# Graph network with LSTM windows: unit 0's gate products ahead of stream 1's last graph product, and two gates ahead of two tanh

## The chip, the cores and the metric

One core of one Trainium2 chip runs the kernel. The metric is the device time in microseconds (us) of one execution; lower is better.

## The reference, cut to what matters

`x` is [64 batches, 128 nodes, 128 features]. Two layers follow one another, each on a layer norm with relu of its input and each added to its input.

```python
h = relu(adj @ (h @ Wg0 + bg0))            # two graph layers, per batch
h = relu(adj @ (h @ Wg1 + bg1))
for p in range(1, 5):                      # windows of p nodes
    wins = h[:, :nw * p, :].reshape(Bv * nw, p, Hd)
    last = lstm_last(Wih[p-1], Whh[p-1], bih[p-1], bhh[p-1], wins)
    h = h.at[:, arange(nw) * p + (p - 1), :].set(last)
# one step of the LSTM:
g = x_t @ Wih.T + h @ Whh.T + bias         # i, f, g, o
c = sigmoid(f) * c + sigmoid(i) * tanh(gg)
h = sigmoid(o) * tanh(c)
# second layer, J = 128 nodes: diagonal, upper and lower part of adj,
# each with weights of its own, summed, plus a bias
```

The windows of one p are independent of one another; those of the next p read what this p wrote.

## The kernel before, in words

The 64 batches run as four groups of 16, and a group as two streams (s = 0, 1) of 8 batches. Every engine has its program written out by hand and waits for semaphores; no planner orders it. The instructions of an engine run in the order of its program.

The graph layers are four products per stream, named after their functions on TensorE: `graph_u` (L418), `graph_z` (L431), `graph_y` (L446) and `graph_v` (L456). Between them other engines take the product out of PSUM: VectorE adds a bias after z (`bias_z`, L910) and after y (`bias_y`, L918). After v, the last product, ScalarE writes the relu rounded to fp32r into HH (`high_h`, L732), and VectorE writes the rest, relu minus HH, into HL (`low_h`, L926). HH and HL together are the LSTM's input. Each of these works on a stream's two banks one after the other.

The LSTM is a list of 22 units, `UNITS` (L32). A unit is one step j of the windows of one p in one stream. For p = 1 each stream has two units of 64 windows (512 columns): units 0 and 2 are stream 0, units 1 and 3 stream 1. Units 4 and 5 are the first step of p = 2, units 6 and 7 the second, and so on. Unit 1 (as unit 0) is the first of its stream: on TensorE (`unit`, L464) it waits for both banks of HH before its first product and for both banks of HL before its third (L470 to L473, L504 to L506).

A unit of p = 1 has three gates (I, C, O; for the first step F is not needed), each of three products of 512 columns: HH by the weights' high part (L500), HH by their low part (L501), HL by the high part (L509). Each gate has its PSUM bank. ScalarE takes gate after gate (L829: sigmoid, or tanh for C, with a bias) into GT and then the tanh of the cell, CS into TC (L835). VectorE computes the cell between them (`unit_cell`, L936; I times C for a first step, L944), then out of the tanh the new hidden value: HH (L977) and HF (L978) for the last step of a window, and HL as HF minus HH (`unit_low`, L992). In group 0, the first, a gate of a new p or chunk waits on ScalarE until the HF of its stream's unit before is written (L812 to L815).

The order on VectorE for the units k (L1106 to L1131): the cell of k unless it was taken early, the hidden value of k, the cell of k + 1 if k + 1 is in `CELL_EARLY` (units 1, 2 and 15), then HL of k. So the cells of units 1 and 2 stand ahead of the HL of units 0 and 1, and the cell of unit 3 behind the HL of unit 2.

TensorE in group 0 starts unit 4 once the HH of unit 2 is written and unit 5 once that of unit 3 is (L491 to L493). Ahead of unit 4 it runs six filling products of ones (L484, 12 records in the profile), which nobody reads.

The stretch around the change, at the start of group 0, before:

- TensorE: y(0), v(0), y(1), v(1) (L621 to L624), then units 0, 1, 2, ...
- ScalarE: HH of stream 0, HH of stream 1 (L803, L804), then the gates and the tanh of unit 0, of unit 1, ...
- VectorE: Y(0), the first bank of HL(0), the first of Y(1), the second of HL(0), the second of Y(1), HL(1) (L1081 to L1086), a wait for the other groups' x (L1087), then the units.

In groups 1 to 3 the units of ScalarE and TensorE run with a plan, an argument that is None in group 0 alone; pieces of the second layer stand between their gates.

Of the kernel before, what the change touches and what calls it, by code (L numbers as in the profile page):

```python
# [9 lines left out]
ACT = mybir.ActivationFunctionType  # L10
# [3 lines left out]
GROUPS = B // G  # L14
HB = G // 2
# [3 lines left out]
HBANKS = HB // PACK  # L19
# [12 lines left out]
def lstm_units():  # L32


    units = []
    for p in SKIPS:
        chunks = max(1, (T // p) * HB // 512)
        nw = (T // p) // chunks
        for c in range(chunks):
            for j in range(p):  # L40
                for s in range(STREAMS):
                    units.append((p, s, j, c * nw, nw, FIRST_STEP if j == 0 else LATER_STEP))
    return units


UNITS = lstm_units()
# [83 lines left out]
LATE_ORDER = ("wi", "wh", "wl", "bias")  # L130

CELL_EARLY = (1, 2, 15)


LN_STATS_AT = {3: range(0, 3), 5: range(3, 5), 6: range(5, 9), 10: range(9, 12), 11: range(12, G)}
# [3 lines left out]
FIRST_STATS_AT = {4 + k: range(3 * k, min(3 * k + 3, G)) for k in range(6)}  # L139
# [5 lines left out]
def program(nc, x_tbd, adj_t, adj_diag, wg0, bg0_col, wg1, bg1, wih_t, whh_t, bih_t, bhh_t, w_l1, bias, out_tbd):  # L145
    with ExitStack() as ctx:
        def sb(name, shape, dt=F32):
            return ctx.enter_context(nc.sbuf_tensor(name, shape, dt))
# [20 lines left out]
        CS = sb("CS", [128, STREAMS, 512])  # L169
        IC = sb("IC", [128, STREAMS, 512])  # L170
        TC = sb("TC", [128, STREAMS, 512])
# [42 lines left out]
        x_rest = sem("x_rest")  # L214
# [34 lines left out]
        cell_ready = sem("cell_ready")  # L249
        tanh_ready = sem("tanh_ready")  # L250
# [20 lines left out]
        def bank(s, n):  # L271
            return PS[:, 4 * s + n, :]
# [144 lines left out]
        def _(pe):  # L417
# [26 lines left out]
            def graph_y(s, g):  # L444

                for n in range(HB):  # L446
                    if n % PACK == 0:
                        pe.wait_ge(h1_ready, 2 * HBANKS * g + s * HBANKS + n // PACK + 1)
                    mm = pe.matmul(as_batches(bank(s, 2 + n // PACK))[:, n % PACK, :],  # L449
                                   Z[:, s, T * n:T * n + T], WG1[:, :], start=True, stop=True)  # L450
                    if n % PACK == PACK - 1:
                        mm.then_inc(y_mm, 1)

            def graph_v(s, g):

                for n in range(HB):  # L456
                    if n % PACK == 0:
                        pe.wait_ge(y_sb, 2 * HBANKS * g + s * HBANKS + n // PACK + 1)
                    mm = pe.matmul(as_batches(bank(s, n // PACK))[:, n % PACK, :],  # L459
                                   Y[:, s, D * n:D * n + D], ADJ[:, :], start=True, stop=True)  # L460
                    if n % PACK == PACK - 1:
                        mm.then_inc(v_mm, 1)
# [158 lines left out]
            graph_y(0, 0)  # L621
            graph_v(0, 0)
            graph_y(1, 0)
            graph_v(1, 0)  # L624

            def units(i, plan):
                for k in range(len(UNITS)):
                    unit(k, i, plan)

            def next_graph(i):  # L630
# [26 lines left out]
            i = GROUPS - 1  # L657
# [54 lines left out]
        def _(act):  # L712
# [19 lines left out]
            def high_h(s, g):  # L732

                for n in range(HBANKS):
                    act.wait_ge(v_mm, 2 * HBANKS * g + s * HBANKS + n + 1)
                    act.activation(HH[:, s, :, n * PACK:(n + 1) * PACK],
                                   as_batches(bank(s, n)).rearrange("p b t -> p t b"),
                                   ACT.Relu).then_inc(h_high, 1)
# [45 lines left out]
            def last_copy(piece, g):  # L784

                if piece.what == TURN:
                    turn_up(g, piece.n, bank(piece.s, F))
                elif piece.what == VALUE:
                    copy_value(g, piece.n, bank(piece.s, F))
# [11 lines left out]
            relu_z(0, 0)  # L801
            relu_z(1, 0)
            high_h(0, 0)  # L803
            high_h(1, 0)  # L804
            act.wait_ge(bias_ready, 1)

            def unit(k, i, plan):

                p, s, j, w0, nw, gates = UNITS[k]
                prev = last_unit(k, s)  # L810
                n = nw * HB
                if plan is None and j == 0 and prev is not None:  # L812


                    act.wait_ge(lstm_step, STEPS * i + STEPS_BEFORE[prev] + STEPS_OF[prev])  # L815
                elif p == 1 and prev is not None:


                    act.wait_ge(lstm_step, STEPS * i + STEPS_BEFORE[prev] + STEPS_OF[prev] - 1)
                if plan and j > 0:  # L820

                    for m in range(len(gates)):
                        for piece in plan.at.get((k, m), ()):
                            last_copy(piece, i - 1)
                for m, q in enumerate(gates):
                    for piece in plan.at.get((k, m), ()) if plan and j == 0 else ():
                        last_copy(piece, i - 1)
                    act.wait_ge(gate_mm, GATES * i + GATES_BEFORE[k] + m + 1)
                    act.activation(GT[:, s, q, 0:n], bank(s, q)[:, 0:n],  # L829
                                   ACT.Tanh if q == C else ACT.Sigmoid,  # L830
                                   bias=BG[:, 4 * (p - 1) + q:4 * (p - 1) + q + 1]).then_inc(gate_act, 1)
                for piece in plan.at.get((k, len(gates)), ()) if plan else ():
                    last_copy(piece, i - 1)
                act.wait_ge(cell_ready, len(UNITS) * i + k + 1)
                act.activation(TC[:, s, 0:n], CS[:, s, 0:n], ACT.Tanh).then_inc(tanh_ready, 1)  # L835

            def units(i, more, plan):
                for k in range(len(UNITS)):
# [22 lines left out]
            i = GROUPS - 1  # L861
# [16 lines left out]
        def _(dve):  # L878
# [39 lines left out]
            def bias_y(s, g, banks=range(HBANKS)):  # L918

                for n in banks:  # L920
                    dve.wait_ge(y_mm, 2 * HBANKS * g + s * HBANKS + n + 1)
                    dve.tensor_tensor(as_batches(Y[:, s, 512 * n:512 * n + 512]), as_batches(bank(s, 2 + n)),
                                      BG1[:, :].unsqueeze(1).broadcast_to([128, PACK, D]),
                                      ALU.add).then_inc(y_sb, 1)

            def low_h(s, g, banks=range(HBANKS)):  # L926

                for n in banks:
                    dve.wait_ge(h_high, 2 * HBANKS * g + s * HBANKS + n + 1)
                    part = slice(n * PACK, (n + 1) * PACK)  # L930
                    dve.scalar_tensor_tensor(out=HL[:, s, :, part],
                                             in0=as_batches(bank(s, n)).rearrange("p b t -> p t b"), scalar=0.0,
                                             in1=HH[:, s, :, part].bitcast(F32),
                                             op0=ALU.max, op1=ALU.subtract).then_inc(h_low, 1)
# [144 lines left out]
            bias_z(0, 0)  # L1079
            bias_z(1, 0)  # L1080
            bias_y(0, 0)  # L1081
            low_h(0, 0, range(1))
            bias_y(1, 0, range(1))
            low_h(0, 0, range(1, HBANKS))
            bias_y(1, 0, range(1, HBANKS))
            low_h(1, 0)  # L1086
            dve.wait_ge(x_rest, 16 * (GROUPS - 1))  # L1087

            def home(plan, what, n):

# [15 lines left out]
            def units(i, more, plan):  # L1106
                for k in range(len(UNITS)):
                    if k not in CELL_EARLY:
                        unit_cell(k, i)
                    for what, q in plan.mid.get(k, ()) if plan else ():  # L1110
                        last_step(what, i - 1, q, plan)
                    stats_at, combine_at, apply_at = (
                        (LN_STATS_AT, LN_COMBINE_AT, LN_APPLY_AT) if plan else
                        (FIRST_STATS_AT, FIRST_COMBINE_AT, FIRST_APPLY_AT))
                    if more and k in stats_at:
                        stats1(i + 1, stats_at[k])
                    if more and k == combine_at:
                        combine(ST1, bn1, G * i + 2 * G, COMBINE * (QUARTERS + 3 * i),
                                MINUS1, VE1, var1, 0, G)
                    if more and k in apply_at:  # L1120
                        norm_h0(i + 1, QUARTERS + i + 1, apply_at[k])
                    unit_hidden(k, i, plan is None)
                    for what, q in plan.between.get(k, ()) if plan else ():
                        last_step(what, i - 1, q, plan)
                    if k + 1 in CELL_EARLY:
                        unit_cell(k + 1, i)
                    unit_low(k, i)
                    for what in LATE_LOW_AT.get(k, ()) if plan is None else ():
                        late_split_low(what)
                    for what, q in plan.late.get(k, ()) if plan else ():  # L1130
                        last_step(what, i - 1, q, plan)  # L1131
# [20 lines left out]
            i = GROUPS - 1  # L1152
# [70 lines left out]
```

## Time and profile before

| | us |
|---|---|
| median of 3 runs | 407.77 (407.67 to 408.24) |
| the profiled execution's own time | 407.99 |
| its span, first to last instruction | 406.2 |
| TensorE busy (matmul records) | 398.6 |
| TensorE weight loads | 347.5 |
| VectorE busy | 338.2 |
| ScalarE busy | 287.5 |
| GpSimd busy | 40.9 |

In the profile PE is TensorE's matmuls, PEld its weight loads, DVE VectorE, ACT ScalarE, POOL GpSimd. Times in rows are from the span's start. A row of the timeline has the start, how long it took (of all of them, if several are merged, "x3"), the engine, the line of the kernel, output and input, and in brackets the idle time ahead with what ended it. A fp32 product of 128 columns gives two records. Matmuls are pipelined: a record of 0.39 us does not keep the next one from starting 0.23 later. In a chain of waits a row is a piece: start, length, what.

### The profile page before, as it was taken

The numbers are of one execution on the slowest core, as the hardware profiler recorded it, in microseconds if no ns is written. First come the engines' busy times: TensorE is split into PE (matmuls) and PEld (weight loads), VectorE is DVE, ScalarE is ACT, GpSimd is POOL, SyncE is SP. The second block draws the span as 40 slices with busy tenths as digits, with TensorE's granted clock in tenths as the row PEclk, the third lists the DMA queues.
The fourth block names the chain that finished last, engine by engine and source line by source line (L and its number), as shares of the span: only waits on it lengthen the run. The fifth ranks groups of instructions, "written<-read, shape, count | busy, mean of one in ns | idle before, by whom it ended". The sixth has DMA issues, their size and how long they took to land.

```text
span 406.2 us, 6535 instructions
## 1 busy us (share of the span) xinstructions
PE 398.6 (98%) x2401; PEld 347.5 (86%) x2401; DVE 338.2 (83%) x858; ACT 287.5 (71%) x579; POOL 40.9 (10%) x43
## 2 busy tenths in 40 slices
PE   8999999999999999999999999999999999999997
PEld 7787889898887889899777889899797788989775
DVE  5668999997989689887998788988898767788795
ACT  4767775685897676777588676777589677766553
POOL 4910003000200003000110000300110000000140
DMA  7820000000000000000000000000000000000003
GB/s 228 310 111 2 1 0 2 1 2 0 2 1 27 1 27 0 27 2 0 3 0 26 27 0 27 1 27 2 0 2 27 26 2 26 2 27 2 1 0 131
DMA packets 5215, 11.18 MB, mean 28 GB/s; under 512 B 1088, under 2 KB 2112, under 8 KB 4672
## 3 DMA queue, kind: packets, MB, share of 16 engines
q1 hardware_dynamic: 5184, 10.77, 7.5%
q8 instruction: 19, 0.31, 0.3%
q14 instruction: 12, 0.10, 0.1%
HBM read 6.57 MB, written 4.19 MB: 27 GB/s over the span
## 4 chain that ended last, share of the span: by engine, by line
PE 84%; DVE 10%; ACT 3%; DMA 1%; issue 1%; POOL 0%; SPq 0%; DVEq 0%; ACTq 0%
PE PS L500 11%; PE PS L509 11%; PE PS L501 11%; PE PS L528 6%; PE PS L573 6%; PE PS L525 6%; PE PS L524 6%; PE PS L449 4%; PE PS L459 4%; PE PS L426 4%; PE PS L441 4%; PE PS L563 3%; PE PS L564 3%; PE PS L565 3%; PE PS L552 2%; ACT TC L835 1%
## 5 line engine op out<-in xcount | busy, mean ns | idle before, releaser
L829 ACT ACTIVATE GT<-PS,BG 128x256 f32<-128x256 f32 (+2 forms) x312 | 158.0, 564 | 17.2 <-PE PS L528 12.0
L500 PE MATMUL PS<-HH,WIH 128*128 128x256 f32 (+2 forms) x312 | 107.8, 346 | 1.7 <-DVE HH L977 1.7
L501 PE MATMUL PS<-HH,WIL 128*128 128x256 f32 (+2 forms) x312 | 102.7, 330 | 0.0
L509 PE MATMUL PS<-HL,WIH 128*128 128x256 f32 (+2 forms) x294 | 97.4, 331 | 0.1
L835 ACT ACTIVATE TC<-CS 128x512 f32<-128x512 f32 (+2 forms) x88 | 45.2, 514 | 49.2 <-DVE CS L953 36.0
L500 PEld LDWEIGHTS PS<-HH,WIH 128*128 128x128 f32 x312 | 58.8, 188 | 10.1 <-DVE HH L984 2.9
L368 POOL TENSOR_TENSOR RS<-VE,NHALF 128x4 f32<-128x4 f32 (+2 forms) x17 | 29.2, 1719 | 353.8 <-DVE VE L901 353.8
L501 PEld LDWEIGHTS PS<-HH,WIL 128*128 128x128 f32 x312 | 58.9, 189 | 4.1 <-issue 1.2
L509 PEld LDWEIGHTS PS<-HL,WIH 128*128 128x128 f32 x294 | 55.5, 189 | 6.1 <-DVE HL L992 1.9
L528 PE MATMUL PS<-SL,WHH 128*128 128x256 f32 (+2 forms) x192 | 60.1, 313 | 0.1
L524 PE MATMUL PS<-SH,WHH 128*128 128x256 f32 (+2 forms) x192 | 59.8, 312 | 0.0
L525 PE MATMUL PS<-SH,WHL 128*128 128x256 f32 (+2 forms) x192 | 59.7, 311 | 0.0
L947 DVE TENSOR_TENSOR IC<-GT 128x256 f32<-128x256 f32 (+2 forms) x48 | 23.8, 496 | 24.5 <-ACT GT L829 24.5
L528 PEld LDWEIGHTS PS<-SL,WHH 128*128 128x128 f32 x192 | 36.3, 189 | 2.1 <-DVE SL L992 0.8
L524 PEld LDWEIGHTS PS<-SH,WHH 128*128 128x128 f32 x192 | 36.3, 189 | 1.4
L525 PEld LDWEIGHTS PS<-SH,WHL 128*128 128x128 f32 x192 | 36.3, 189 | 1.3
L980 DVE TENSOR_TENSOR HT<-GT,TC 128x256 f32<-128x256 f32 (+2 forms) x48 | 23.7, 494 | 6.4 <-ACT TC L835 5.4
L944 DVE TENSOR_TENSOR CS<-GT 128x512 f32<-128x512 f32 (+2 forms) x40 | 23.9, 597 | 3.8 <-ACT GT L829 3.8
L772 ACT ACTIVATE WH<-PS,RS 128x384 f32<-128x384 f32 x32 | 17.8, 580 | 10.7 <-PE PS L565 10.2
L953 DVE TENSOR_TENSOR CS<-IC,CS 128x256 f32<-128x256 f32 (+2 forms) x48 | 23.9, 497 | 1.7
L992 DVE TENSOR_TENSOR SL<-HT,SH 128x256 fp32r<-128x256 f32 (+2 forms) x48 | 23.9, 497 | 1.5
L980 DVE TENSOR_TENSOR HF<-GT,TC 128x512 f32<-128x512 f32 (+2 forms) x32 | 18.9, 592 | 6.9 <-ACT TC L835 6.2
(96 smaller groups left out, 652.8 us busy)
## 6 DMA issues: line engine op xcount, KB each, us to landing
out_tbd<-X SPq DMA_DIRECT2D x15, 256.0 KB, 2.0
X<-x_tbd SPq DMA_DIRECT2D x3, 1024.0 KB, 12.9
X<-x_tbd SPq DMA_DIRECT2D x4, 256.0 KB, 4.5
WI<-wih_t SPq DMA_DIRECT2D x1, 1024.0 KB, 5.8
WH<-whh_t SPq DMA_DIRECT2D x1, 768.0 KB, 7.3
out_tbd<-X SPq DMA_DIRECT2D x2, 128.0 KB, 1.7
WL<-w_l SPq DMA_DIRECT2D x1, 192.0 KB, 6.5
WG<-wg SPq DMA_DIRECT2D x2, 64.0 KB, 3.4
```

The lines of the kernel that those rows point to most:

```text
L368: pool.tensor_tensor(rs[:, lo:hi], ve[:, lo:hi], NHALF[:, lo:hi], ALU.pow).then_inc(done, 1)
L500: pe.matmul(dst, WIH[:, p - 1, cols], x_high, start=True, stop=False)
L501: pe.matmul(dst, WIL[:, p - 1, cols], x_high, start=False, stop=False)
L509: mm = pe.matmul(dst, WIH[:, p - 1, cols], x_low, start=False, stop=(j == 0))
L524: pe.matmul(dst, WHH[:, p - 2, cols], SH[:, s, 0:n], start=False, stop=False)
L525: pe.matmul(dst, WHL[:, p - 2, cols], SH[:, s, 0:n], start=False, stop=False)
L528: pe.matmul(dst, WHH[:, p - 2, cols], SL[:, s, 0:n], start=False, stop=True).then_inc(gate_mm, 1)
L573: mm = pe.matmul(ps[:, lo * D:hi * D], ADJ2[:, k, :], values(q)[:, 1 + k, lo * D:hi * D], start=False, stop=(k == SIDES - 1))
L829: act.activation(GT[:, s, q, 0:n], bank(s, q)[:, 0:n], ACT.Tanh if q == C else ACT.Sigmoid, bias=BG[:, 4 * (p - 1) + q:4 * (p - 1) + q + 1 ...
L835: act.activation(TC[:, s, 0:n], CS[:, s, 0:n], ACT.Tanh).then_inc(tanh_ready, 1)
L944: dve.tensor_tensor(CS[:, s, 0:n], GT[:, s, I, 0:n], GT[:, s, C, 0:n], ALU.mult).then_inc(cell_ready, 1)
L980: dve.tensor_tensor(full, o, tc, ALU.mult).then_inc(lstm_step, 1)
```

## The change

TensorE runs unit 0 between y(1) and v(1). ScalarE takes unit 0's three gates ahead of HH of stream 1, and the tanh of unit 0 behind it. The tanh of a unit becomes a function, `tanh_c`; for units 1 and 2 in group 0 (`TANH_LATE`) it is called behind the first gate of the next unit rather than behind the unit's own last gate. VectorE takes both banks of HL(0), then both of Y(1), and HL(1) behind the cell of unit 0; its wait for the other groups' x stands at unit 4, ahead of their first use. Nothing is added or left out of the work.

```diff
--- before.py
+++ after.py
@@ -130,6 +130,8 @@
 LATE_ORDER = ("wi", "wh", "wl", "bias")
 
 CELL_EARLY = (1, 2, 15)
+
+TANH_LATE = (1, 2)
 
 
 LN_STATS_AT = {3: range(0, 3), 5: range(3, 5), 6: range(5, 9), 10: range(9, 12), 11: range(12, G)}
@@ -621,10 +623,11 @@
             graph_y(0, 0)
             graph_v(0, 0)
             graph_y(1, 0)
+            unit(0, 0, None)
             graph_v(1, 0)
 
             def units(i, plan):
-                for k in range(len(UNITS)):
+                for k in range(0 if plan else 1, len(UNITS)):
                     unit(k, i, plan)
 
             def next_graph(i):
@@ -801,8 +804,14 @@
             relu_z(0, 0)
             relu_z(1, 0)
             high_h(0, 0)
-            high_h(1, 0)
             act.wait_ge(bias_ready, 1)
+
+            def tanh_c(k, i):
+
+                p, s, j, w0, nw, gates = UNITS[k]
+                n = nw * HB
+                act.wait_ge(cell_ready, len(UNITS) * i + k + 1)
+                act.activation(TC[:, s, 0:n], CS[:, s, 0:n], ACT.Tanh).then_inc(tanh_ready, 1)
 
             def unit(k, i, plan):
 
@@ -825,14 +834,18 @@
                 for m, q in enumerate(gates):
                     for piece in plan.at.get((k, m), ()) if plan and j == 0 else ():
                         last_copy(piece, i - 1)
+                    if plan is None and m == 1 and k - 1 in TANH_LATE:
+                        tanh_c(k - 1, i)
                     act.wait_ge(gate_mm, GATES * i + GATES_BEFORE[k] + m + 1)
                     act.activation(GT[:, s, q, 0:n], bank(s, q)[:, 0:n],
                                    ACT.Tanh if q == C else ACT.Sigmoid,
                                    bias=BG[:, 4 * (p - 1) + q:4 * (p - 1) + q + 1]).then_inc(gate_act, 1)
                 for piece in plan.at.get((k, len(gates)), ()) if plan else ():
                     last_copy(piece, i - 1)
-                act.wait_ge(cell_ready, len(UNITS) * i + k + 1)
-                act.activation(TC[:, s, 0:n], CS[:, s, 0:n], ACT.Tanh).then_inc(tanh_ready, 1)
+                if plan is None and k == 0:
+                    high_h(1, 0)
+                if plan or k not in TANH_LATE:
+                    tanh_c(k, i)
 
             def units(i, more, plan):
                 for k in range(len(UNITS)):
@@ -1079,12 +1092,8 @@
             bias_z(0, 0)
             bias_z(1, 0)
             bias_y(0, 0)
-            low_h(0, 0, range(1))
-            bias_y(1, 0, range(1))
-            low_h(0, 0, range(1, HBANKS))
-            bias_y(1, 0, range(1, HBANKS))
-            low_h(1, 0)
-            dve.wait_ge(x_rest, 16 * (GROUPS - 1))
+            low_h(0, 0)
+            bias_y(1, 0)
 
             def home(plan, what, n):
 
@@ -1107,11 +1116,15 @@
                 for k in range(len(UNITS)):
                     if k not in CELL_EARLY:
                         unit_cell(k, i)
+                    if plan is None and k == 0:
+                        low_h(1, 0)
                     for what, q in plan.mid.get(k, ()) if plan else ():
                         last_step(what, i - 1, q, plan)
                     stats_at, combine_at, apply_at = (
                         (LN_STATS_AT, LN_COMBINE_AT, LN_APPLY_AT) if plan else
                         (FIRST_STATS_AT, FIRST_COMBINE_AT, FIRST_APPLY_AT))
+                    if plan is None and k == min(FIRST_STATS_AT):
+                        dve.wait_ge(x_rest, 16 * (GROUPS - 1))
                     if more and k in stats_at:
                         stats1(i + 1, stats_at[k])
                     if more and k == combine_at:
```

## Rows read from the trace of the kernel before

**Rows 1.** Busy us (and count) by stretch: PE, PEld, DVE, ACT, POOL, PEclk, DMA share.

```profile
24.80:38.00 13.20, 12.24 (x61) 9.85 (x60) 10.21 (x17) 11.12 (x19) 0.00 (x0) 1.00 0.00 2
38.00:49.40 11.40, 11.40 (x49) 9.36 (x50) 10.87 (x24) 7.84 (x13) 0.00 (x0) 1.00 0.01 2
49.40:74.40 25.00, 24.10 (x155) 22.72 (x154) 22.79 (x59) 17.02 (x37) 3.09 (x1) 1.00 0.00 1
74.40:95.00 20.60, 20.58 (x169) 20.18 (x170) 18.10 (x53) 15.68 (x41) 0.00 (x0) 1.00 0.00 1
```

**Rows 2.** The chain of waits from 28 to 38 us: start, length, what.

```profile
28.08 0.64 ACT TC L835
...
28.74 0.69 DVE HH L977
29.43 0.60 DVE HF L978
30.04 0.61 DVE CS L944
...
30.67 0.64 ACT TC L835
...
33.27 0.64 ACT TC L835
...
35.26 0.69 DVE HL L992
...
36.59 0.64 ACT TC L835
...
37.25 0.70 DVE HH L977
```

**Rows 3.** The timeline of TensorE, 22.7 to 38.2 us.

```profile
22.78 2.35 PE L459 MATMUL PS<-ADJ,Y 128*128 128x128 f32 x16
24.89 0.47 PE L500 MATMUL PS<-HH,WIH 128*128 128x512 f32 x1
...
25.43 0.40 PE L509 MATMUL PS<-HL,WIH 128*128 128x512 f32 x1
...
27.51 0.39 PE L509 MATMUL PS<-HL,WIH 128*128 128x512 f32 x1
...
33.17 1.50 PE L484 MATMUL PS<-ONES 128*128 128x128 f32 x12
34.68 0.50 PE L500 MATMUL PS<-HH,WIH 128*128 128x512 f32 x1
...
38.00 0.50 PE L500 MATMUL PS<-HH,WIH 128*128 128x512 f32 x1 [0.95 <-DVE HH L977]
```

**Rows 4.** The timeline of ScalarE, 20 to 31 us.

```profile
20.25 0.60 ACT L736 ACTIVATE HH<-PS 128x512 fp32r<-128x512 f32 x1 [1.48 <-PE PS L459]
21.14 0.60 ACT L736 ACTIVATE HH<-PS 128x512 fp32r<-128x512 f32 x1 [0.29 <-PE PS L459]
23.97 0.60 ACT L736 ACTIVATE HH<-PS 128x512 fp32r<-128x512 f32 x1 [2.24 <-PE PS L459]
...
25.93 2.01 ACT L829 ACTIVATE GT<-PS,BG 128x512 f32<-128x512 f32 x3 [0.16 <-PE PS L509]
...
28.61 1.83 ACT L829 ACTIVATE GT<-PS,BG 128x512 f32<-128x512 f32 x3
30.67 0.63 ACT L835 ACTIVATE TC<-CS 128x512 f32<-128x512 f32 x1 [0.23 <-DVE CS L944]
```

**Rows 5.** The timeline of VectorE, 25 to 30 us.

```profile
25.80 0.69 DVE L931 SCALAR_TENSOR_TENSOR HL<-PS,HH 128x512 fp32r<-128x512 f32 x1 [0.50 <-ACT HH L736]
27.35 0.69 DVE L944 TENSOR_TENSOR CS<-GT 128x512 f32<-128x512 f32 x1 [0.86 <-ACT GT L829]
...
29.95 0.68 DVE L944 TENSOR_TENSOR CS<-GT 128x512 f32<-128x512 f32 x1
```

**Rows 6.** The timeline of TensorE, 1.0 to 4.2 us.

```profile
1.05 3.57 PE L611 MATMUL PS<-ONES 128*128 128x128 f32 x15 [1.05 <-POOL NHALF L356]
```

## The prediction

> **What bounds the kernel now.** I read the stretches first [rows 1]. The profiled execution spans 406.2 us and its own time is 407.99 us. From 38.0 to 49.4 us TensorE is busy without a gap, and from 49.4 to 95 us it lacks 0.9 us in all. The stretch that the change touches, 24.8 to 38.0, is the one with room: 12.24 busy of 13.20. All instructions of group 0 follow one another and nothing in them waits for a time of day (the last loads are in: the DMA share of this stretch is 0.00), so a shift at 38.0 is a shift of the end. TensorE is not what sets 38.0.
>
> The chain of waits over 28 to 38 us [rows 2] shows what does. It is a ladder of ScalarE and VectorE: tanh of the cell (L835), HH (L977), HF (L978), the next unit's cell CS (L944), the next tanh. The tanh of units 0 to 3 start at 28.08, 30.67, 33.27 and 36.59. Two steps are 2.60 us; the last is 3.32, since HL (L992) of unit 2 stands ahead of unit 3's cell in VectorE's order. The HH of unit 3 starts at 37.25, and TensorE starts unit 5 at 38.00 after 0.95 idle [rows 3]. TensorE is ahead of the ladder: it is through unit 3 at 33.17 and runs 12 filling records (1.50) until the HH of unit 2 lets unit 4 go at 34.68.
>
> So the question is when the ladder's steps come, above all tanh 0 and tanh 1, and whether the new order makes them sooner.
>
> **The change, part by part.**
>
> TensorE, unit 0 ahead of v(1). Stream 1's last product starts at 22.78 and unit 0 at 24.89 [rows 3]. Unit 0 now takes the place at 22.78, 2.11 us sooner. Its inputs stand: stream 0's HH is written by 21.74 (21.14 + 0.60 [rows 4]), and its second HL, no longer behind a bias addition, right after that, by about 22.5, where the third product comes at 23.3. Nine products take 2.08 (25.43 to 27.51 for the third product of units 0 and 1 [rows 3]), and v(1) starts where unit 1 started less 2.11, at 24.94 (27.51 - 0.46 for two products - 2.11).
>
> Here a rule and a row differ. The row gives 0.23 us from product to product at 512 columns. The Trainium skill (TensorE: Matmul & The Clock Gate, Back-to-back issue gap) states about 131 ns per product of 512 columns as the sustained rate; unit 0 would then hold v(1) up by some 1.2 us, the first term below would vanish, and the sum would be 408.4. The row, with this kernel's own operands, decides.
>
> VectorE, bias_y and low_h in whole calls. Y(1) now waits for the second HL(0): by HL's and its own slots of 0.6 I put it at 22.4 and 23.0, so it ends at 23.7, and v(1) reads it from 24.94. Cost nothing; the cover is unit 0 on TensorE. Were v(1) next, the first Y would be some 0.4 late. The wait for the other groups' x moves to unit 4 and is met in both places. The wait for the biases on ScalarE is long met.
>
> ScalarE, high_h(1) behind unit 0's gates. The gates come 2.11 sooner: 25.93 becomes 23.82, and the three end at 25.83 (2.01 [rows 4]). v(1) released its first HH 1.19 after its start (22.78, 23.97), and the second bank comes 0.89 after the first (20.25, 21.14) [rows 4]: HH(1) starts at 26.13 and 27.02 and is written at 27.62. Tanh 0, whose cell is done by 26.0 (27.35 - 2.11 + 0.69 [rows 5]), stands behind both and starts at 27.6 instead of 28.08. So of 2.1 us that unit 0 is sooner, 0.5 is left at tanh 0. The HH of unit 0 then waits for HL(1) on VectorE too and starts at 28.3 (28.74 before).
>
> Who waits for HH(1) and HL(1): unit 1 on TensorE, its first product for all of HH(1) (27.68), its third for all of HL(1). The second HL starts at 27.65 and takes 0.69 [rows 5]: 28.34. So TensorE stands from 26.9 to 27.68 and again shortly, and the third product starts at 28.40 (27.51 before). A product that was waited for takes 0.10 longer (0.50 at 34.68 against 0.40 [rows 3]), and a gate starts 0.50 after its third product (25.43, 25.93 [rows 3, 4]). Gate 1 of unit 1 is at 29.00 (28.61 before). The third products follow at 29.20 and 29.90, the gates at 29.70 and 30.40: ScalarE is paced by TensorE here, where before it was the other way round. Unit 1's cell needs the second gate: 29.70 + 0.63 + 0.03 = 30.36, against 29.95 [rows 5]. **First term: +0.41 us.**
>
> ScalarE, a gate ahead of tanh 1. It needs unit 2's first product group, whose third product is at 29.90 + 0.69 = 30.59, so the gate starts at 31.09 and tanh 1 one slot of 0.60 later (three gates in 1.83 [rows 4]) at 31.69. Without this edit tanh 1 would start at 31.08, once the cell is written (30.36 + 0.68 + 0.04). **Second term: +0.61.** Tanh 1 is at 31.69 against 30.67 [rows 4]: +1.02. What the edit can buy is ScalarE time, of which there was 0.23 idle ahead of tanh 1 [rows 4]; nobody on the ladder waits for that.
>
> ScalarE, a gate ahead of tanh 2. The ladder gives tanh 2 at 31.69 + 2.60 = 34.29. The gate ahead (unit 3) waits for unit 1's HF, written at 31.69 + 0.67 + 0.61 + 0.69 = 33.66, starts at 33.70, and tanh 2 at 34.30. Cost 0.01; it hides beside unit 2's cell on VectorE.
>
> After that: tanh 3 at 34.30 + 3.32 = 37.62 and the HH of unit 3 at 38.28, 1.03 later than before. TensorE: units 1 to 3 end at 34.2, the fill at 35.7, the HH of unit 2 is written at 35.66, so unit 4 starts at 35.7 and is done by 38.0, while unit 5 waits for 39.03. The fill costs nothing beside that; were the ladder faster, it and unit 4 would hold unit 5 until about 37.9. That floor says that even a perfect ladder gains 0.1 us at unit 5.
>
> **Sum:** 0.41 + 0.61 + 0.01 = 1.03 us. The profiled execution would go from 407.99 to 409.0; the median of the runs is 0.22 below it, so 407.77 becomes 408.8.
>
> What the trace does not show, bounded: unit 0's products directly ahead of v(1) on TensorE, from 0 to one product's slot, 0.23, late (nearest: the change of kind the other way round, ahead of 24.89, where two steps take 0.54 instead of 0.46 [rows 3]; it is near the lower end, so I take 0); the first HH behind v(1), which before was itself waited for, from 1.09 to 1.19 (the 0.10 of a stalled product; I take 1.19, its own row); the stalled third product, from 0 to twice its row, 0.20 (I take 0.10). Together -0.2 to +0.33 on the sum: 408.6 to 409.1.
>
> **The rivals.**
>
> A, the gate ahead of tanh 1 is free. If unit 1's gates were early enough for the first gate of unit 2 to end before unit 1's cell is written, or if ScalarE took tanh 1 first all the same, only the first term would stay: 408.2. For it: ScalarE did idle 0.23 there. Against it: TensorE delivers that gate's input at 31.09, after the cell. A chain 0.3 shorter than mine up to HL(1), with half the slot hidden, is of the same kind: 408.4 to 408.5. Chance 0.22.
>
> B, not slower: the head start carries. Tanh 0 is 0.5 sooner, and if every later step kept its 2.60, 2.60 and 3.32, the HH of unit 3 would come at 36.8 and the time would be 407.3, or 407.7 with the floor by fill and unit 4. It decides at HL(1): it must be written by about 27.5, so that unit 1's third product is not later than now. Against it: HL(1) now stands behind unit 0's 2.1 us and v(1) on TensorE, and was written at 26.49 before (25.80 + 0.69 [rows 5]). The Trainium skill (Perfetto Trace Analysis, Optimization Strategy) says to find the gaps of the most-contended engine and make what they wait for start sooner; by that the 0.95 us gap ahead of unit 5 would shrink and this case would hold. Chance 0.12.
>
> C, the clock. TensorE would now stand for 0.8 us and again 0.2 within two microseconds. If it fell to the lower of its two levels (1.2 of 2.4 GHz), units 2 and 3 would run at 0.46 a product, 18 x 0.23 = 4.1 us more: 413. The filling records at the start show that pace (15 records in 3.57 us, 0.24 each [rows 6], against 12 in 1.50, 0.125 each, at 33.17 [rows 3]). Against it: 0.95 us idle ahead of 38.00 was followed by products at full pace. The same page on TensorE (The HAM clock gate, of the Trainium skill) says that idleness lowers the clock; the row on 38.00 shows that a gap of this size does not. Chance 0.02.
>
> **How the numbers follow.** My case has 0.64. A difference under about 0.2% (0.8 us) can't be told from none. My case lies at 408.6 to 409.1, nearly all of it slower by over 0.2%; 0.05 of it falls under the bound. A is no change. B is mostly no change; for faster by over 0.2% it would have to gain 0.8, more than its own price, which leaves 0.05. Slower: 0.59 + 0.02 for C + 0.05 from A's upper end = 0.66. Faster 0.05, same 0.29. The range takes my case and most of A: 408.0 to 409.3, and leaves out B, C and the tails, near 0.2.
>
> **What would show it.** In the changed profile: unit 0's first product at 22.8; HH(1) written near 27.6; unit 1's third product at 28.4; tanh 1 at 31.7, right behind a gate; HH of unit 3 at 38.3; unit 5 at 39.0 after an idle of about 1 us; and everything behind it as long as before. I am wrong if tanh 1 starts by 31.1 (then A), if unit 5 starts by 38.0 (then B), or if the part behind unit 5 changes its length.

## The result, and the profile after

The changed kernel takes **408.92 us** (median of 8 runs, 408.59 to 409.34), the kernel before 407.78 in the runs beside it (407.47 to 408.24). The ratio is 1.0028, interval 1.0019 to 1.0038: slower by 1.14 us. The forecast was 408.8, slower.

The profiled execution of the changed kernel has a span of 406.7 us and a time of 408.65. Its start must be set apart first: when the first loads land differs from one execution to the next, and the first HH of stream 0 on ScalarE started at 20.25 us before and at 19.70 here. Up to that instruction the two programs are the same, so these 0.55 us are chance. From here on I give moments **from the start of that first HH** ("after HH"), and the stretch from unit 5's first product to the end of the span as "the rest". The span is given to 0.1 us, so a rest is good to 0.05.

The busy time by stretch of the changed kernel (columns as in [rows 1]), cut at the same events:

```profile
24.25:38.15 13.90, 12.26 (x66) 9.77 (x64) 10.41 (x17) 10.83 (x19) 0.00 (x0) 1.00 0.00 1
38.15:49.55 11.40, 11.40 (x49) 9.35 (x50) 10.87 (x24) 7.84 (x13) 0.00 (x0) 1.00 0.01 2
49.55:74.55 25.00, 24.08 (x154) 22.70 (x153) 22.79 (x59) 16.98 (x36) 3.09 (x1) 1.00 0.00 1
74.55:95.15 20.60, 20.59 (x169) 20.19 (x170) 18.10 (x53) 15.67 (x41) 0.00 (x0) 1.00 0.00 1
```

The three stretches behind unit 5 are those of before to 0.02 us. The granted clock is 1.00 in all four, its upper level. The difference lies ahead of 38.15, and, as shown below, in one more place.

The chain of waits of the changed kernel, to be laid beside [rows 2]:

```profile
26.23 0.61 ACT HH L739
...
26.88 0.50 PE PS L502
...
27.62 0.50 PE PS L511
...
28.14 2.05 ACT GT L840 x3
...
30.24 0.69 ACT GT L840
30.93 0.53 ACT TC L814
...
31.48 0.69 DVE HH L990
32.18 0.61 DVE HF L991
...
32.81 0.69 ACT GT L840
33.50 0.55 ACT TC L814
...
34.08 0.69 DVE HH L990
34.77 0.61 DVE HF L991
...
35.41 0.69 DVE HL L1005
36.10 0.61 DVE CS L957
...
36.73 0.64 ACT TC L814
...
37.40 0.70 DVE HH L990
...
38.15 0.50 PE PS L502
```

Before, the ladder was tanh, HH, HF, cell, tanh. Now its lower end is HH(1), then unit 1's products, its three gates, and a fourth gate, which is unit 2's and stands ahead of tanh 1. From tanh 1 on the steps are the old ones, 2.58 and 3.32 us.

The timeline of TensorE in the changed kernel [rows 3]:

```profile
22.10 0.48 PE L502 MATMUL PS<-HH,WIH 128*128 128x512 f32 x1
...
24.25 1.95 PE L461 MATMUL PS<-ADJ,Y 128*128 128x128 f32 x16
26.88 0.50 PE L502 MATMUL PS<-HH,WIH 128*128 128x512 f32 x1 [0.69 <-ACT HH L739]
...
27.61 0.50 PE L511 MATMUL PS<-HL,WIH 128*128 128x512 f32 x1
...
38.15 0.50 PE L502 MATMUL PS<-HH,WIH 128*128 128x512 f32 x1 [0.95 <-DVE HH L990]
```

Unit 0 starts at 2.40 after HH, where it was at 4.64 (24.89 - 20.25). For that v(1) starts at 4.55 instead of 2.53 (24.25 - 19.70, 22.78 - 20.25), 2.02 later, and TensorE stands 0.69 ahead of unit 1; the gap of 0.95 ahead of unit 5 is as large as it was. ScalarE [rows 4]:

```profile
23.14 2.00 ACT L840 ACTIVATE GT<-PS,BG 128x512 f32<-128x512 f32 x3 [1.95 <-PE PS L511]
25.34 0.60 ACT L739 ACTIVATE HH<-PS 128x512 fp32r<-128x512 f32 x1 [0.20 <-PE PS L461]
26.23 0.60 ACT L739 ACTIVATE HH<-PS 128x512 fp32r<-128x512 f32 x1 [0.29 <-PE PS L461]
26.73 0.62 ACT L814 ACTIVATE TC<-CS 128x512 f32<-128x512 f32 x1
28.14 2.79 ACT L840 ACTIVATE GT<-PS,BG 128x512 f32<-128x512 f32 x4 [0.79 <-PE PS L511]
30.83 0.62 ACT L814 ACTIVATE TC<-CS 128x512 f32<-128x512 f32 x1
```

Tanh 0 is 0.80 sooner than before (7.03 after HH, was 7.83), tanh 1 is 0.71 later (11.13, was 10.42), unit 5 is 0.70 later (18.45, was 17.75).

**The second place.** 0.70 is not 1.14. The rest is 368.55 us (406.7 - 38.15) where it was 368.20 (406.2 - 38.00). It was made in the last 25 us, in this part of VectorE's timeline, first of the kernel before, then of the changed one:

```profile
382.67 0.68 DVE L999 TENSOR_TENSOR X<-PS,X 128x512 f32<-128x512 f32 x1
383.45 0.87 DVE L1024 BATCH_NORM_STATS2 ST<-X 128x6 f32<-128x128 f32 x4
384.24 0.67 DVE L1040 SCALAR_TENSOR_TENSOR HTL<-PS,HTH 128x512 fp32r<-128x512 f32 x1
```

```profile
382.82 0.69 DVE L1012 TENSOR_TENSOR X<-PS,X 128x512 f32<-128x512 f32 x1
383.97 0.87 DVE L1037 BATCH_NORM_STATS2 ST<-X 128x6 f32<-128x128 f32 x4 [0.46 <-DVE X L1012]
384.75 0.67 DVE L1053 SCALAR_TENSOR_TENSOR HTL<-PS,HTH 128x512 fp32r<-128x512 f32 x1
```

The statistics wait for nothing but the addition that VectorE itself has just done (and for a load that landed at the start). Before, they started 0.10 after its end, now 0.46. HTL, which stands behind them and which TensorE waits for, is late by the same 0.36. The trace of the changed kernel has 6534 instructions where that of before has 6535, and the missing one is VectorE's (896 and 897): VectorE's wait for the other groups' x was a second wait on unit 0's cell, which costs an instruction of its own, and is the only one on the statistics of unit 4. So everything behind lies one place earlier in VectorE's program. That this is the cause was a guess until the experiments.

0.70 + 0.35 = 1.05 us, against 1.14 in the medians. The last 0.09 is left open.

### The profile page after: what moved, and what is told of

It is laid out like the page before. It is cut to its first block, busy times and chain, and to the rows that moved or that the text cites. A ratio compares the mean times of both kernels' runs of the same rounds, so it can differ in the third digit from the quotient of the medians.

```text
span 406.7 us, 6534 instructions
## 1 busy us (share of the span) xinstructions
PE 398.5 (98%) x2401; PEld 347.2 (85%) x2401; DVE 338.3 (83%) x858; ACT 287.7 (71%) x579; POOL 40.9 (10%) x43
## 4 chain that ended last, share of the span: by engine, by line
PE 84%; DVE 10%; ACT 3%; DMA 1%; issue 1%; POOL 0%; SPq 0%; DVEq 0%; ACTq 0%
PE PS L502 11%; PE PS L511 11%; PE PS L503 11%; PE PS L530 6%; PE PS L575 6%; PE PS L527 6%; PE PS L526 6%; PE PS L451 4%; PE PS L428 4%; PE PS L461 4%; PE PS L443 4%; PE PS L565 3%; PE PS L566 3%; PE PS L567 3%; ACT GT L840 2%; PE PS L554 2%
```

## The experiments

Each was timed in five rounds, 7 to 12 runs, beside the kernel before. Moments are from one profile each.

| kernel | tanh 1 after HH | unit 5 after HH | rest | median us | ratio to before |
|---|---|---|---|---|---|
| before | 10.42 | 17.75 | 368.20 | 407.78 | |
| changed | 11.13 | 18.45 | 368.55 | 408.92 | 1.0028 (1.0019 to 1.0038) |
| e1, changed, no late gate | 10.60 | 17.93 | 368.43 | 408.28 | 1.0014 (1.0005 to 1.0023) |
| e7, changed, late gate of tanh 2 alone | 10.62 | 18.17 | 368.54 | 408.43 | 1.0022 (1.0014 to 1.0031) |
| e8, as e1, tanh 0 ahead of HH(1) | 10.69 | 18.02 | 368.62 | 408.25 | 1.0013 (1.0005 to 1.0022) |
| e9, changed, x wait back | 11.15 | 18.47 | 368.19 | 408.63 | 1.0020 (1.0011 to 1.0029) |
| e2, before, late gates alone | 10.64 | 17.98 | 368.22 | 408.00 | 1.0007 (0.9998 to 1.0015) |
| e4, before, VectorE's order alone | 10.46 | 17.79 | 368.22 | 407.99 | 1.0001 (0.9992 to 1.0010) |
| e10, before, x wait moved alone | 10.35 | 17.68 | 368.50 | 408.09 | 1.0008 (0.9999 to 1.0016) |
| e11, as e10, one more instruction | 10.36 | 17.68 | 368.19 | 407.59 | 1.0000 (0.9991 to 1.0008) |
| e12, before, one more instruction | 10.44 | 17.77 | 368.23 | 407.50 | 0.9997 (0.9988 to 1.0006) |
| e3, before, cell 3 early | 10.42 | 17.04 | 368.13 | 407.04 | 0.9985 (0.9976 to 0.9993) |
| e5, unit 0 split around v(1) | 9.92 | 17.25 | 368.20 | 407.06 | 0.9985 (0.9976 to 0.9994) |
| e6, e5 and cell 3 early | 9.91 | 16.53 | 368.26 | **406.70** | 0.9972 (0.9962 to 0.9983) |

The kernel before had a median of 407.75 beside e1, e2, e3 and e7, 407.85 beside e4, e6, e9 and e10, and 407.67 beside the other four. So the ratios, the moments and the rests compare better than the medians.

### e1: the changed kernel without late gates

```diff
-TANH_LATE = (1, 2)
+TANH_LATE = ()
```

> The changed kernel with TANH_LATE empty: unit 0 stays ahead of v(1), tanh 1 and tanh 2 stand ahead of the next unit's gates again. All times here from the start of stream 0's first HH (ScalarE), which leaves out when the first loads land. Theory L (two terms on the ladder, the larger from the late gate): tanh 1 starts 0.55 sooner than with the change (10.56 after HH against 11.13), as soon as unit 1's cell is written, and unit 5 at 17.9 against 18.45 with the change and 17.75 before; time 0.55 below the changed kernel, 408.3 to 408.5, or 0.1 to 0.2 over before if the end of the kernel adds nothing. Rival S (all of the cost is v(1) behind unit 0, the gate ahead of tanh 1 is free): unit 5 stays at 18.4 and the time at 408.9. Rival E (0.35 of the cost is made in the last 25 us, by where the program lies): the stretch from unit 5's first product to the end stays 368.5 as with the change, against 368.2 before.

Tanh 1 at 10.60, unit 5 at 17.93, 408.28: theory L held, to 0.04 us. The chain of waits in this kernel shows what is left of the first term:

```profile
28.59 0.69 ACT GT L840
...
29.29 0.70 ACT GT L840
...
30.01 0.70 DVE CS L957
...
30.74 0.65 ACT TC L814
```

Tanh 1 starts as soon as unit 1's cell is written, and that is set by unit 1's second gate. Unit 0 ahead of v(1) costs 0.18 at unit 5, the late gates 0.52. The rest stays long, at 368.43, as rival E had it: nothing in the late gates makes it.

### e7: the gate ahead of tanh 2 alone

```diff
-TANH_LATE = (1, 2)
+TANH_LATE = (2,)
```

> The changed kernel with the gate ahead of tanh 2 alone (TANH_LATE of unit 2 only). Theory L: the gate ahead of tanh 2 fits beside unit 2's cell, so the ladder is that of the kernel without any late gate to 0.05 us: tanh 2 some 13.15 after the first HH, unit 5 at 17.9, time as that kernel's. Rival S2 (a gate put ahead of a tanh costs its slot of 0.6 wherever it stands): unit 5 at 18.4 to 18.5 and the time 0.5 above the kernel without a late gate.

Neither. Unit 5 is at 18.17, 0.24 later than in e1. I had looked at what the gate waits for (unit 1's HF) and not at ScalarE's own load: from a tanh in its old place to the next behind a late gate it must do three gates, the gate and then the tanh. Its timeline:

```profile
30.41 0.63 ACT L814 ACTIVATE TC<-CS 128x512 f32<-128x512 f32 x1
30.94 2.40 ACT L840 ACTIVATE GT<-PS,BG 128x512 f32<-128x512 f32 x4
33.22 0.64 ACT L814 ACTIVATE TC<-CS 128x512 f32<-128x512 f32 x1
```

That is 2.81 us from tanh to tanh, with no idle time in it, against a ladder step of 2.60. So a gate put ahead of a tanh is paid where ScalarE's order shifts by one place. In the change that is tanh 1; between tanh 1 and tanh 2 ScalarE has again three gates to do, and tanh 2 costs nothing (2.58 from the one to the other).

### e2: the late gates in the kernel before

```diff
+TANH_LATE = (1, 2)
@@
+                    if plan is None and m == 1 and k - 1 in TANH_LATE:
+                        tanh_c(k - 1, i)
                     act.wait_ge(gate_mm, GATES * i + GATES_BEFORE[k] + m + 1)
@@
+                if plan or k not in TANH_LATE:
+                    tanh_c(k, i)
```

> The kernel before with the gates ahead of tanh 1 and tanh 2 alone; unit 0 behind v(1) as before. Theory L: the gate of unit 2 can start when unit 1's third gate ends (its products and unit 0's HF are there 0.4 earlier), tanh 1 comes one slot later less the 0.23 that ScalarE idled there: 0.35 later than before, so 10.77 after the first HH; tanh 2 adds nothing; unit 5 at 18.1 against 17.75, time 408.1. Rival S (the late gate is free, ScalarE works on in the idle time): unit 5 at 17.75 and 407.8. A gain would show the late gate is worth something in the order it was not combined with.

Tanh 1 and unit 5 come 0.22 and 0.23 later, in time 0.25 over the kernel before, though the interval just takes in no change. The moments show it, the time does not settle it.

The 0.22 is less than the 0.35 that I expected. On ScalarE gates start 0.57 apart here (four steps from 28.07 to the tanh at 30.34 take 2.27). In the kernel before, the next start would have been free at about 30.32 (three such steps from 28.61), and tanh 1 came at 30.67: the engine had 0.35 to give, not the 0.23 that the row calls idle, since the row counts from the end of the last gate and not from the next possible start. 0.57 less 0.35 is 0.22. In the change almost the whole slot is paid (0.53 at tanh 1, 0.52 at unit 5), since TensorE lets the gate go at 10.54 after HH, only 0.06 ahead of the moment at which tanh 1 starts without it.

### e8: tanh 0 ahead of HH(1)

```diff
-                if plan is None and k == 0:
-                    high_h(1, 0)
                 if plan or k not in TANH_LATE:
                     tanh_c(k, i)
+                if plan is None and k == 0:
+                    high_h(1, 0)
```

(with TANH_LATE empty)

> The changed kernel without late gates, and with tanh 0 ahead of HH(1) on ScalarE rather than behind it. Theory L (HL(1) sets unit 1, and with it tanh 1; when tanh 0 comes does not matter): tanh 0 starts 1.5 sooner, at 5.5 after the first HH, HH(1) starts 0.4 later for its first bank and no later for its second, the second HL(1) 0.1 later, tanh 1 at 10.7 against 10.60, unit 5 at 18.0, time 408.3 to 408.4. Rival (tanh 0's place behind HH(1) is what eats the head start): tanh 1 at 10.0 or sooner and unit 5 at 17.4, time 407.8.

Tanh 0 starts at 5.52 after HH (25.18 - 19.66) instead of 7.03, and nothing follows from it: tanh 1 at 10.69, unit 5 at 18.02. What eats the head start of unit 0 is not that tanh 0 stands behind HH(1), but that unit 1 is late.

### e5 and e6: unit 0 split, and cell 3 early

```diff
-            unit(0, 0, None)
+            unit(0, 0, None, (0, 1))
             graph_v(1, 0)
+            unit(0, 0, None, (2,))
@@ ScalarE, unit 0, ahead of its gate O
+                    if plan is None and k == 0 and m == 2:
+                        high_h(1, 0)
+                        tanh_c(0, i)
@@ VectorE, hidden value of unit 0
+                if direct and k == 0:
+                    dve.wait_ge(gate_act, 3)
```

e6 adds on VectorE, as e3 does on the kernel before:

```diff
-                    if k not in CELL_EARLY:
+                    if k not in CELL_EARLY and not (plan is None and k == 3):
                         unit_cell(k, i)
@@
-                    if k + 1 in CELL_EARLY:
+                    if k + 1 in CELL_EARLY or (plan is None and k + 1 == 3):
                         unit_cell(k + 1, i)
```

The expectations of e5, e3 and e6 follow in this order; the "combined kernel" in the first is e6.

> Unit 0 split around v(1) as in the combined kernel, without late gates, cell of unit 3 where it was. Theory L: tanh 1 at 9.9 after the first HH as in the combined kernel, then steps of 2.60 and 3.32: unit 5 at 17.2 to 17.3 against 17.75 before; time 407.3. It says what the early products can give once unit 1 is not made late by them. Rival (all of the combined kernel's gain came from unit 3's cell): unit 5 at 17.7, time 407.8.

> The kernel before with one other edit in group 0: the cell of unit 3 ahead of HL of unit 2 on VectorE, so that the last step of the ladder is 2.60 as the others instead of 3.32. Theory L (the start of unit 5 sets the end one for one): tanh 3 0.7 sooner, HL of unit 2 0.6 later, which unit 4 meets with a stall of 0.4; unit 5 at 17.1 after the first HH against 17.75, time 407.1 to 407.2. Rival (the ladder isn't what sets the end, or unit 4 takes over): unit 5 at 17.5 or later, time 407.5 to 407.8.

> The changed kernel without late gates, with unit 0 split on TensorE: its gates I and C ahead of v(1), its gate O behind it, in the time that TensorE stood waiting for HH(1); ScalarE takes I, C, HH(1), tanh 0, O; VectorE's hidden value of unit 0 waits for O; and the cell of unit 3 ahead of HL of unit 2 in group 0. Theory L: v(1), HH(1) and HL(1) come 0.69 sooner than with the change, so unit 1's third product is at its place of before and the head start of tanh 0 is kept: tanh 1 some 9.8 after the first HH against 10.42 before; with the last step 2.60 the ladder would put unit 5 at 16.4, but fill and unit 4 on TensorE hold it to about 16.6. Time 406.6 to 406.9 with the wait for x moved (0.35 of it from the end). Rival (unit 1 stays late whatever the order, or TensorE's fill and unit 4 take all of it): unit 5 at 17.1 or later, no better than the kernel before with cell 3 alone, 407.0 and above.

In group 0 all three came as theory L had them: unit 5 at 17.25, 17.04 and 16.53, times 407.06, 407.04 and 406.70. One term of e6's sum did not come: with the wait for x moved I had put 0.35 at the end, and the rest is 368.26. The reason is in the edit: the new wait for gate O is an instruction of its own on VectorE (897 in e5 and e6, as before the change), so what follows lies in its old place.

Unit 1's third product, in e5:

```profile
27.19 0.50 PE L513 MATMUL PS<-HL,WIH 128*128 128x512 f32 x1
```

That is 7.24 after HH, where it was at 7.26 before (27.51 - 20.25) and at 7.91 with the change (27.61 - 19.70). In e6 the chain of waits from v(1) to unit 5 has TensorE alone:

```profile
24.14 1.78 PE PS L461 x16
...
26.62 0.49 PE PS L504
...
27.35 0.49 PE PS L513
...
33.30 1.34 PE PS L486 x12
...
36.04 0.76 PE PS L520 x3
36.80 0.32 PE PS L504
```

So early products of unit 0 are worth 0.5 us (17.75 to 17.25) once the third gate fills the gap behind v(1) and HH(1) comes 0.7 sooner than in the change. The early cell of unit 3 is worth another 0.7. In e3 TensorE has no gap left ahead of unit 5 (0.95 before): unit 4's last three products, which wait for unit 2's HL, and the ladder are there at the same moment, to 0.02 us. e6 beats both kernels, by 1.15 us beside the kernel before. Two of the pieces above, the first and the third product of unit 1, still start within 0.06 us after HH(1) and HL(1) are written; from the third on TensorE works without a gap, with the filling records among its work.

### e9 to e12: the rest

e9 puts the wait back in the changed kernel; e10 moves it in the kernel before and does nothing else:

```diff
 e9:
             bias_y(1, 0)
+            dve.wait_ge(x_rest, 16 * (GROUPS - 1))
@@
-                    if plan is None and k == min(FIRST_STATS_AT):
-                        dve.wait_ge(x_rest, 16 * (GROUPS - 1))
 e10:
-            dve.wait_ge(x_rest, 16 * (GROUPS - 1))
@@
+                    if plan is None and k == min(FIRST_STATS_AT):
+                        dve.wait_ge(x_rest, 16 * (GROUPS - 1))
```

The expectations of e9 and e10:

> The changed kernel with VectorE's wait for the other groups' x put back ahead of the units, where the kernel before has it. On unit 0's cell this wait is a second one and costs an instruction of its own; on the statistics at unit 4 it does not, so the changed program of VectorE is one instruction shorter and everything behind lies one place earlier. Theory E (0.35 us of the cost is made in the last 25 us, at the statistics of the second bank on VectorE, which stand 0.46 idle behind the addition of x in the three kernels with the wait moved and not in the three without): the idle time is gone and the stretch from unit 5's first product to the end is 368.2 instead of 368.5; the ladder is as with the change (unit 5 at 18.45 after the first HH); time 0.35 below the changed kernel: 408.5. Rival (the stall comes with the order of HL and Y or with the times at which things arrive): the stretch stays 368.5, time 408.9.

> The kernel before with nothing but VectorE's wait for the other groups' x moved to unit 4. Theory E: nothing changes in group 0 (unit 5 at 17.75 after the first HH), but the statistics of the second bank near the end stand 0.46 idle and the stretch from unit 5 to the end is 368.5; time 0.35 over before: 408.1. Rival: no difference, 407.75.

The rest is 368.19 in e9 and 368.50 in e10, with the stall of 0.46 at the same statistics in e10:

```profile
382.17 0.68 DVE L999 TENSOR_TENSOR X<-PS,X 128x512 f32<-128x512 f32 x1
383.31 0.87 DVE L1024 BATCH_NORM_STATS2 ST<-X 128x6 f32<-128x128 f32 x4 [0.46 <-DVE X L999]
```

In time e9 is 0.29 below the changed kernel; e10 is 0.24 over the kernel before, less than its interval can settle. e9 also shows something I had got wrong. With unit 0 early, the wait in its old place is not met:

```profile
26.02 0.69 DVE L957 TENSOR_TENSOR CS<-GT 128x512 f32<-128x512 f32 x1 [2.58 <-DMA X<-x_tbd]
27.46 0.47 PE L502 MATMUL PS<-HH,WIH 128*128 128x512 f32 x1 [0.93 <-DVE HL L944]
```

Unit 0's cell stands until 26.02 for loads that only later units need; in the kernel before the last of them landed at 26.43, and the cell started at 27.35 [rows 5], later than that. Tanh 0 did not suffer, since it stands behind HH(1) until 27.07. HL(1), behind the cell on VectorE, did: unit 1's first product, which waits for the first bank of HL(1) as well (L475 of the changed kernel), started 7.42 after HH instead of 7.18. At tanh 1 0.02 of it is left. An order with an earlier tanh 0 or HL(1) needs the wait moved.

e11 and e12 ask whether it is the place in the program or the way group 0 ran. e11 is e10, e12 the kernel before, each with one more wait, long met, ahead of the last group:

```diff
             i = GROUPS - 1
+            dve.wait_ge(x_quarter[0], 16)
             units(i, False, LATE)
```

Their expectations:

> The kernel before with VectorE's wait for the other groups' x moved to unit 4, and one more wait on VectorE, long met, ahead of group 3's first cell, which costs one instruction. Theory P (the stall of 0.46 near the end comes from where that stretch lies in VectorE's program): the extra instruction puts the stretch back in its place of before, although nothing is changed near it and group 0 stays as with the wait moved: no idle time at the second statistics, 368.2 from unit 5 to the end, time 407.7. Rival G (the stall comes from how group 0 ran): stall and 368.5 stay, time 408.1.

> The kernel before with that one extra met wait ahead of group 3's first cell and nothing else, so the stretch near the end lies one place later than before. Theory P says only that the last stretch may change; if any shift costs something, it is longer than 368.2 by 0.2 to 0.5 and a row on VectorE shows an idle time that the kernel before lacks; if the place of before is not special, it stays 368.2 and the time 407.8. Group 0 as before, unit 5 at 17.75.

e11 has the rest of before, 368.19, and no idle time at the statistics:

```profile
381.87 0.68 DVE L999 TENSOR_TENSOR X<-PS,X 128x512 f32<-128x512 f32 x1
382.66 0.87 DVE L1024 BATCH_NORM_STATS2 ST<-X 128x6 f32<-128x128 f32 x4
```

One instruction that does nothing, more than 80 us ahead of the stall and in another group than the edit, takes it away: it hangs on where that stretch lies in VectorE's program. One place later than before (e12) costs nothing. VectorE's order of HL(0) and Y(1) has no part in it and none in the ladder:

```diff
-            low_h(0, 0, range(1))
-            bias_y(1, 0, range(1))
-            low_h(0, 0, range(1, HBANKS))
-            bias_y(1, 0, range(1, HBANKS))
+            low_h(0, 0)
+            bias_y(1, 0)
```

> The kernel before with VectorE's new order alone: both banks of HL(0), then both of Y(1), the wait for x where it was. Unit 0 still stands behind v(1), so the first Y(1) is what TensorE waits for and comes 0.38 later, the second 0.2 sooner. Theory L: v(1) starts 0.4 later but no longer stands in its middle, so unit 0 starts within 0.15 of before, and tanh 0 and unit 5 with it: unit 5 at 17.75 to 17.9, time 407.75 to 407.9, and the last stretch 368.2. Rival (the cover of Y(1) is worth its 0.38): unit 5 at 18.1, time 408.1.

That is e4. Unit 5 at 17.79, the rest 368.22, ratio 1.0001.

Not tried: unit 1 without its wait for HL(1), which would be a race.

## Why the prediction was right, and where it was wrong

The time and its sign were right (408.8 forecast, 408.92 measured). That it came so near is luck: two errors of a third of a microsecond stood against each other. Unit 5 was forecast 1.03 later and came 0.70 later, and 0.35 that the sum did not have was added at the end. My own last sign of being wrong, a change in the length of the part behind unit 5, came true.

**What bounds the kernel.** Right for the ladder. The start of unit 5 moves the end one for one: e3, e5 and e6 move it by -0.71, -0.50 and -1.22, and the rest stays within 0.07 of before in all three. One premise was misread: the loads were not all in by 24.8. The DMA share of the whole stretch rounds to 0.00, but the last load of x landed at 26.43. Before, nothing waited for it; in e9 unit 0's cell does.

**Unit 0 ahead of v(1), first term 0.41.** The mechanism was right (HL(1) makes unit 1 late, its second gate sets the cell and the cell tanh 1), the size was not: 0.18 by e1. Three small prices were each at the wrong end. Unit 0 starts 2.40 after HH and not 2.53, since TensorE was free of y(1) before Y(1) let v(1) go at 22.78. The first HH(1) comes 1.09 after v(1) (24.25, 25.34): the lower end of my bound, where I took the price of a v(1) that had itself been waited for. The gate starts 0.53 after a stalled third product (27.61, 28.14), not 0.60. Together 0.30 at unit 1's first gate; 0.23 of it is left at tanh 1 (10.60 in e1, where I had 31.08 - 20.25 = 10.83).

**The gate ahead of tanh 1, second term 0.61.** Measured 0.52 (e1 to changed). Right in kind. The slot itself was right (0.59 from the gate at 30.24 to tanh 1 at 30.83). What was off is when the gate starts beside the moment at which tanh 1 comes without it: I had it 0.01 behind that moment (31.09, 31.08), and it was 0.06 ahead of it (10.54 and 10.60 after HH).

**The gate ahead of tanh 2, 0.01.** Right for the change: the gate waits for unit 1's HF (32.81) and is through when unit 2's cell is written. The reason was incomplete, as e7 shows. It leaves out ScalarE's own load, which is light enough only because the gate ahead of tanh 1 has already been paid for.

**VectorE's order.** Right: 0.04 by e4.

**The step that failed** is the one that puts the move of the wait for x at nothing, since it "is met in both places". The move takes an instruction out of VectorE's program, and 0.35 us appeared some 345 us behind unit 5. The sentence that "a shift at 38.0 is a shift of the end" is true of time and not of place. The trace of before shows the extra instruction (at 27.28, ahead of unit 0's cell), but nothing in it could have shown the stall; a range that leaves room for a change of the program's length would have been the honest one.

**The rivals.** A (the late gate is free) fell with e1: without the gates unit 5 is 0.52 sooner. B (the head start carries) fell for the change, and e8 shows that tanh 0 is not the place to save it; e5 shows the condition that it named, HL(1) in time, to be the right one. The rule of the Trainium skill behind B (Perfetto Trace Analysis, Optimization Strategy) agrees with e5 and e6, where the gap ahead of unit 5 went from 0.95 to 0.61 and to nothing, and not with the change: there it stayed at 0.95 and one of 0.69 was added. The length of a gap alone does not tell: in e1 it is 0.61 as well, and unit 5 comes 0.18 later than before. C (the clock) fell: after both gaps the first step is 0.34 and the next are 0.23 us, but for the stalled third product.

The other page weighed ahead of the sum (the Trainium skill, TensorE: Matmul & The Clock Gate, Back-to-back issue gap) would have made unit 0 hold v(1) up by 1.2 us. The trace disagrees again: the products of unit 0 and v(1) lie at 22.10 and 24.25, 2.15 apart.

## What to carry to other kernels

To run a unit's work earlier, ask first what it pushes back: here one stream's head start of 2.2 us on TensorE made the other stream's unit the late one, and the same idea gained 0.5 once the pushed work fitted a gap. A slot put ahead of the work on the critical ladder costs its length less what the engine had to spare there, and that is counted from start to start, not from the idle time in a row: 0.22 of 0.57 was paid in e2, nearly all in the change. It is paid once, where the order shifts. When two edits of 0.2 to 0.5 us are compared, count the instructions of each engine too, and look at the whole trace, not at the stretch that was edited.

## What the runs showed of the hardware that I had not expected

A stretch of VectorE's program that lies one instruction earlier stalled for 0.46 us at one instruction whose waits were met (0.10 otherwise), in all five kernels that have it there (changed, e1, e7, e8, e10) and in none of the nine others. e5 and e6 are among the nine: their wait for x is moved as well, but one more wait stands in its stead. The rest is 368.43 to 368.62 us in the five and 368.13 to 368.26 in the nine. One extra met wait, ahead of group 3's first cell, takes the stall away (e11). What VectorE does in that time stays open.

The Trainium skill (Runtime: NRT & Kernel Launch, Instruction fetch mechanics) says that each engine's instructions are brought in in blocks of 256 while earlier ones run. A stall bound to a place would fit a block's edge. The profiles do show loads of instructions, as DMA queues of that kind; the one that bears on this is, in the kernel before:

```profile
q14 instruction: 12, 0.10, 0.1%
```

In the traces one of its packets, of 8 KB, lies at this place. In the nine kernels without the stall it starts 0.48 to 0.75 us after the addition does, and so ahead of the statistics. In the five with it, it starts 1.81 or 1.82 after the addition, and so 0.66 to 0.68 behind the start of the statistics. So the stall and the time of an instruction load change together. But this packet comes when the stall is over, and the trace does not say which engine it is for: that a load is the cause is not shown.

The extra wait on unit 0's cell has a price of its own where it stands: without it (e10, e11) tanh 0, tanh 1 and unit 5 come 0.07 sooner.
